# Mixture-of-experts layer: token rows of experts 3 to 7 turned by block transposes of VectorE instead of by TensorE and a PSUM copy

## The reference, cut to what matters

```python
h = h + attention(layernorm(h))          # h: [592, 256]
x = layernorm(h)
red = x @ w_red
wg_n = wg / jnp.maximum(jnp.linalg.norm(wg, axis=1, keepdims=True), 0.0001)
gates = jax.nn.softmax(red @ wg_n.T, axis=1)
idx = jnp.argmax(gates, axis=1)          # one expert of eight for each token
scores = jnp.take_along_axis(gates, idx[:, None], axis=1)
hid = gelu(einsum('td,edf->etf', x, w1) + b1)   # w1: [8, 256, 1024]
y = einsum('etf,efd->etd', hid, w2) + b2        # w2: [8, 1024, 256]
out = h + y[idx] * scores
```

## Time and profile before

| | |
|---|---|
| runs | 129.05 us median, 128.87 to 130.22 |
| profiled execution: its own time | 129.21 us |
| its span in the trace | 127.4 us, so 1.8 us lie around the span |
| mean granted clock of TensorE | 0.994 |
| PE busy / weight loads busy | 121.1 us (95%) / 102.5 us (80%) |
| DVE / ACT / POOL busy | 57.4 / 48.2 / 43.8 us |
| DMA | 32.75 MB, 257 GB/s over the span |

### The profile page before, as it was taken

How to read it: one execution, slowest core, us unless ns; L and a number is a source line. 1 busy time by engine, 2 the same in 40 slices (tenths; PEclk the granted TensorE clock), 3 DMA queues, 4 the chain that set the end, 5 groups by cost and what they waited for, 6 DMA issues and landing times.

```text
span 127.4 us, 3630 instructions
## 1 busy us (share of the span) xinstructions
PE 121.1 (95%) x1492; PEld 102.5 (80%) x1492; DVE 57.4 (45%) x181; ACT 48.2 (38%) x145; POOL 43.8 (34%) x59
## 2 busy tenths in 40 slices
PE   7999999999999999999999899999999999999970
PEld 2677888877667777788799798899898999999870
DVE  1140699581997858798887200160212121220220
ACT  0400002465575757575547660037233150606000
POOL 8800024590059029563858700032020202002052
PEclk9999999999999999999999999999999999999997
DMA  3999999139819999999999947999999999300011
GB/s 114 309 315 391 400 402 408 57 126 207 145 28 205 153 277 363 386 368 378 366 403 367 373 151 219 289 286 363 368 384 373 375 385 357 97 5 25 3 29 31
DMA packets 19697, 32.75 MB, mean 257 GB/s; under 512 B 1794, under 2 KB 13701, under 8 KB 19678
## 3 DMA queue, kind: packets, MB, share of 16 engines
q1 hardware_dynamic: 18126, 30.06, 73.2%
q0 software_dynamic: 784, 2.12, 4.6%
q10 hardware_dynamic: 768, 0.31, 0.9%
HBM read 27.41 MB, written 5.38 MB: 257 GB/s over the span
## 4 chain that ended last, share of the span: by engine, by line
PE 85%; DVE 5%; DMA 3%; issue 2%; POOL 1%; ACT 1%; POOLq 0%; SPq 0%; DVEq 0%
PE ps L838 20%; PE ps L854 19%; PE ps L548 11%; PE ps L695 5%; PE ps L609 4%; PE ps L708 4%; PE ps L739 4%; PE ps L602 4%; PE ps L677 4%; DMA early<-embed_in 3%; PE ps L702 2%; PE ps L819 2%; PE ps L635 2%; DVE wide L942 2%; PE ps L808 1%
## 5 line engine op out<-in xcount | busy, mean ns | idle before, releaser
L530 ACT ACTIVATE early<-ps,b1s 128x112 f32<-128x112 f32 x64 | 17.4, 355 | 30.4 <-PE ps L838 30.4
L838 PE MATMUL ps<-early,w1s 128*64 128x112 f32 x512 | 26.1, 259 | 0.5 <-issue 0.5
L838 PEld LDWEIGHTS ps<-early,w1s 128*64 128x64 f32 x512 | 25.6, 137 | 1.0 <-issue 0.8
L854 PE MATMUL ps<-w2s,early 128*64 128x256 f32 x224 | 25.7, 379 | 0.0
L854 PEld LDWEIGHTS ps<-w2s,early 128*64 128x64 f32 x224 | 20.0, 130 | 3.2
L548 PE MATMUL ps<-early 128*128 128x256 f32 x60 | 15.9, 415 | 0.2
L548 PEld LDWEIGHTS ps<-early 128*128 128x128 f32 x60 | 11.8, 205 | 3.5 <-DMA early<-embed_in 2.0
L1126 DVE COPY early<-ps 128x224 f32<-128x224 f32 x6 | 2.4, 392 | 24.4 <-PE ps L819 24.4
L1271 POOL DMA_INDIRECT out<-pos,early x4 | 3.8, 944 | 24.7 <-DVE pos L1144 24.4
L609 PE MATMUL ps<-xnt,wqkv 128*128 128x296 f32 x32 | 9.1, 422 | 0.0
L1271 POOL DMA_INDIRECT out<-pos,wide x3 | 2.9, 980 | 17.5 <-DVE pos L1144 17.5
(11 more groups left out here) (148 smaller groups left out, 183.4 us busy)
## 6 DMA issues: line engine op xcount, KB each, us to landing
w1s<-w SPq DMA_DIRECT2D x8, 1024.0 KB, 10.1
w2s<-w SPq DMA_DIRECT2D x8, 1024.0 KB, 12.8
early<-embed_in SPq DMA_DIRECT2D x5, 448.0 KB, 7.7
slot_scratch<-nil SPq DMA_DIRECT2D x1, 2240.0 KB, 14.1
early<-slot_scratch SPq DMA_DIRECT2D x4, 280.0 KB, 4.0
wide<-slot_scratch SPq DMA_DIRECT2D x4, 280.0 KB, 6.6
b2s<-b SPq DMA_DIRECT2D x4, 256.0 KB, 7.9
wqkv<-w_qkv SPq DMA_DIRECT2D x1, 768.0 KB, 10.9
```

The lines of the kernel that those rows point to most:

```text
L530: nc.scalar.activation(gt[:, t % 2, f, :], ps[:, 2 * (t % 2) + f // 4, (f % 4) * CAP:(f % 4 + 1) * CAP], ACT.Gelu, bias=b1t[:, f:f + 1]).t ...
L838: m = nc.tensor.matmul(ps[a * ROW_B:(a + 1) * ROW_B, 2 * (t % 2) + f // 4, (f % 4) * CAP:(f % 4 + 1) * CAP], w1s[:, r, k, c:c + ROW_B], xt ...
L854: m = nc.tensor.matmul(ps[n0:n1, 4 + t % 2, 0:D], gt[:, t % 2, f, n0:n1], w2s[:, r, f, :], start=(f == 0), stop=(f == FT - 1))
```

## The change

The identity matmuls and the PSUM copy stay for expert 2 alone, now inside down(1) before f = 6, into PSUM bank 0 (`turn_rows(ONCHIP)`). For experts 3 to 7 PE turns nothing. `rows_turned(t)` on DVE waits for the rows themselves and issues 16 transposes: each takes 32 token rows and, in one instruction, two blocks of 32 channels (one of each half of 128 channels), and writes a block [32 channels, 2, 32 tokens] of `xt`. `xt` becomes 128 tokens wide instead of 112. The row loads and the clearing take 128 rows of each expert instead of 112, so that the transposes read defined rows. Matmuls still use 112 tokens. down_halves no longer waits for `xt_ready`.

```diff
+QB = 32
+NQ = P // QB
...
-        xt = late(2 * KD * CAP).rearrange("p (b k n) -> p b k n", b=2, k=KD)
+        xt = late(2 * KD * P).rearrange("p (b k n) -> p b k n", b=2, k=KD)
...
+        def block_rows(t):
+            r = t % E
+            return rows[:, r, :] if r < RING else more[:, r - RING, :]
+
         def row_of(t):
-            r = t % E
-            return rows[0:CAP, r, :] if r < RING else more[0:CAP, r - RING, :]
+            return block_rows(t)[0:CAP, :]
...
-            sp.dma_start(of_expert[0:CAP, :, :], nil[0:CAP, :].unsqueeze(1).to_broadcast([CAP, E, ROW]))\
+            sp.dma_start(of_expert[0:P, :, :], nil[:, :].unsqueeze(1).to_broadcast([P, E, ROW]))\
               .then_inc(q["slots_cleared"], 16)
...
             def load_rows(t):
-                sp.dma_start(row_of(t), of_expert[0:CAP, t, :]).then_inc(gathered[t], 16)
+                sp.dma_start(block_rows(t), of_expert[0:P, t, :]).then_inc(gathered[t], 16)
...
             def turn_rows(t):
-                pe.wait_ge(gathered[t % E], 16 * (t // E + 1))
-                if t >= ONCHIP + 2:
-                    pe.wait_ge(q["xt_ready"], t - ONCHIP - 1)
+                pe.wait_ge(gathered[t], 16)
+                pe.wait_ge(q["gelu_ready"], FT * (t - 1))
...
-                        m = nc.tensor.matmul(ps[a * ROW_B:(a + 1) * ROW_B, 6 + t % 2, k * CAP:(k + 1) * CAP],
+                        m = nc.tensor.matmul(ps[a * ROW_B:(a + 1) * ROW_B, 0, k * CAP:(k + 1) * CAP],
...
                 for f in range(FT):
-                    if t == 1 and f == FT // 2:
-                        turn_rows(2)
+                    if t == 1 and f == FT - 2:
+                        turn_rows(ONCHIP)
...
             down(0)
             down(1)
-            turn_rows(3)
             hidden(2)
             for t in range(3, E):
                 hidden(t)
-                if t + 1 < E:
-                    turn_rows(t + 1)
                 down(t - 1)
...
             def rows_turned(t):
-                dve.wait_ge(q["xt_ps"], t - ONCHIP + 1)
+                dve.wait_ge(gathered[t % E], 16 * (t // E + 1))
                 dve.wait_ge(q["hidden_ps"], 2 * (t - 1))
-                V.tensor_copy(xt[:, t % 2, :, :],
-                              ps[:, 6 + t % 2, 0:KD * CAP].rearrange("p (k n) -> p k n", k=KD))\
-                    .then_inc(q["xt_ready"], 1)
+                z = block_rows(t)[:, D:2 * D].rearrange("p (k b) -> p k b", k=KD)
+                for i in range(NQ):
+                    for b in range(NQ):
+                        m = V.transpose(xt[b * QB:(b + 1) * QB, t % 2, :, i * QB:(i + 1) * QB],
+                                        z[i * QB:(i + 1) * QB, :, b * QB:(b + 1) * QB])
+                m.then_inc(q["xt_ready"], 1)
...
-            rows_turned(2)
+            dve.wait_ge(q["xt_ps"], 1)
+            V.tensor_copy(xt[:, 0, :, 0:CAP], ps[:, 0, 0:KD * CAP].rearrange("p (k n) -> p k n", k=KD)).then_inc(q["xt_ready"], 1)
             rows_turned(3)
             result(0)
             result(1)
```

More of the change, by code:

```diff
@@ L379, in _ @@
                 for i in range(OVF):
-                    sp.dma_start(of_expert[(i + 1) * CAP:(i + 2) * CAP, :, :], nil[0:CAP, :].unsqueeze(1).to_broadcast([CAP, E, ROW]))\
+                    sp.dma_start(of_expert[(i + 1) * P:(i + 2) * P, :, :], nil[:, :].unsqueeze(1).to_broadcast([P, E, ROW]))\
                       .then_inc(q["spill_cleared"], 16)
@@ L385, in _ @@
                     e = sp.value_load(meta[0:1, i:i + 1], min_val=0, max_val=E - 1)
-                    row = sp.value_load(meta[0:1, OVF + i:OVF + i + 1], min_val=0, max_val=(E + 1) * APART - CAP)
+                    row = sp.value_load(meta[0:1, OVF + i:OVF + i + 1], min_val=0, max_val=(E + 1) * APART - P)
                     r = (E + i) % RING
@@ L397, in _ @@
                     sp.wait_ge(scattered[i % 2], 16 * (i // 2 + 1))
-                    sp.dma_start(row_of(E + i), slot_d[bass.ds(row, CAP), :]).then_inc(gathered[i], 16)
+                    sp.dma_start(block_rows(E + i), slot_d[bass.ds(row, P), :]).then_inc(gathered[i], 16)
             sp.wait_ge(scattered[0], 16 * E // 2)
@@ L515, in _ @@
                 act.wait_ge(q["soon_ps"], KD * t + 1)
-                nc.scalar.activation(xt[:, t, 0, :], ps[:, BX[t][0], 0:CAP], ACT.Copy).then_inc(q["soon0_ready"], 1)
+                nc.scalar.activation(xt[:, t, 0, 0:CAP], ps[:, BX[t][0], 0:CAP], ACT.Copy).then_inc(q["soon0_ready"], 1)
             act.wait_ge(q["low_ready"], 1)
@@ L800, in down_halves @@
                 pe.wait_ge(q["y_ready"], t - 1)
-                pe.wait_ge(q["xt_ready"], t - ONCHIP + 1)
                 for h, bank in ((0, BHALF), (1, 4 + t % 2)):
@@ L839, in hidden @@
                                 ps[a * ROW_B:(a + 1) * ROW_B, 2 * (t % 2) + f // 4, (f % 4) * CAP:(f % 4 + 1) * CAP],
-                                w1s[:, r, k, c:c + ROW_B], xt[:, t % 2, k, :], start=(k == 0), stop=(k == KD - 1))
+                                w1s[:, r, k, c:c + ROW_B], xt[:, t % 2, k, 0:CAP], start=(k == 0), stop=(k == KD - 1))
                     if f % 4 == 3:
@@ L874, in _ @@
                     with pe.If(n > i):
-                        turn_rows(E + i)
                         hidden(E + i)
@@ L1096, in _ @@
                 dve.wait_ge(q["soon_ps"], KD * (t + 1))
-                V.tensor_copy(xt[:, t, 1, :], ps[:, BX[t][1], 0:CAP]).then_inc(q["soon1_ready"], 1)
+                V.tensor_copy(xt[:, t, 1, 0:CAP], ps[:, BX[t][1], 0:CAP]).then_inc(q["soon1_ready"], 1)
             scores_of(BY_PE, NT)
@@ L1119, in overflow @@
                 link(V.scalar_tensor_tensor(orow[:, :], obase[:, :], -float(CAP), orow[:, :], ALU.mult, ALU.add))
-                V.tensor_scalar(meta[:, OVF:2 * OVF], orow[:, :], float((E + 1) * APART - CAP), None, ALU.min)\
+                V.tensor_scalar(meta[:, OVF:2 * OVF], orow[:, :], float((E + 1) * APART - P), None, ALU.min)\
                     .then_inc(q["meta_ready"], 1)
             def rows_turned(t):
-                dve.wait_ge(q["xt_ps"], t - ONCHIP + 1)
+                dve.wait_ge(gathered[t % E], 16 * (t // E + 1))
                 dve.wait_ge(q["hidden_ps"], 2 * (t - 1))
-                V.tensor_copy(xt[:, t % 2, :, :],
-                              ps[:, 6 + t % 2, 0:KD * CAP].rearrange("p (k n) -> p k n", k=KD))\
-                    .then_inc(q["xt_ready"], 1)
+                z = block_rows(t)[:, D:2 * D].rearrange("p (k b) -> p k b", k=KD)
[4 more added lines that the diff above has]
+                m.then_inc(q["xt_ready"], 1)
             def result(t):
```

## The result

| | before | changed |
|---|---|---|
| median of 20 runs | 129.44 us | 128.66 us |
| ratio to before, 95% interval | | 0.9935 (0.991 to 0.996) |
| profiled execution, its span | 129.21, 127.4 | 129.17, 127.4 |

The change made the kernel faster by 0.65%, 0.84 us. The twenty runs of the kernel before, the first three of which the prediction started from, have a median 0.39 us above that of the three; the ratio applied to 129.05 would give 128.2, inside the range. But the gain is under half of the one forecast.

A forecast was written before the change was run, and what follows sets the result against it. The prediction took PE, busy 121.1 of 127.4 us and without a wait in the experts' stage, to bound the kernel. Its terms, -1.95 + 0.15 = -1.8 us, gave 127.3 us, range 126.7 to 128.6.

The forecast's parts named there:

- 1.95 us off TensorE: Experts' stage: removing turn_rows of experts 3 to 7 from PE, five times 0.39 us, saves 1.95 us.
- The start of hidden(2), 0.15 us: Before hidden(2): expert 2's copy has less PE work to cover it, costing 0.15 us more.
- The transposes of expert 3: Before hidden(3): 16 DVE transposes at 0.137 us take 2.2 us, ending 0.9 us before wanted; nothing on the path.
- 16 d - 3.1: Before hidden(3): PE's wait in us if the cover fails, with d the cost of one transpose.
- the first rival: Before hidden(3): transposes don't overlap, perhaps because a transposer fills before emptying; one wait of 0.6 to 1.1 us; chance 0.15.
- (N + 151)/0.96 ns: Expert 3's transposes: skill's tensor_tensor formula, estimating 0.224 us each; one behind another, a 0.5 us wait, run 127.8 us.
- Experts 4 to 7, nothing: Later periods: DVE needs 3.2 of 6.5 us for transposes and result steps, so nothing is added.
- DMA, nothing on the path: Clearing and row loads widened to 128 rows: clearing at most 1 us longer, weights covered by at least 0.7 us; nothing added.

The follow-up runs named there:

- e8: The changed kernel plus three extra transposes of 32, 128 or 256 elements behind those of experts 4 to 7; mean start distances 0.12, 0.22 and 0.35 us.
- e9: The changed kernel plus three extra transposes (unshifted, 128 partitions, bf16) or plain copies of 64 elements behind experts 4 to 7's; transposes start 0.145 us apart on the mean.
- e4: The changed kernel with one block transpose per expert instead of 16; ratio 0.9865 to the kernel before, stretch 45.67 us.
- e1: The changed kernel with clearing and row loads of 112 rows as before; ratio 0.9919 to the kernel before, stretch 46.16 us.
- e2: The kernel before with only the clearing and row loads widened to 128 rows; ratio 1.0021 to the kernel before, stretch 47.51 us.
- e13: The changed kernel with expert 2's copy on ScalarE, 112-row transfers and the two transpose loops swapped; ratio 0.9881 to the kernel before, stretch 44.72 us.
- e3: The changed kernel with expert 2's copy of turned rows on ScalarE instead of VectorE; ratio 0.9883 to the kernel before, stretch 45.58 us.
- e11: The changed kernel plus three extra 64-element transposes behind experts 4 to 7's; output, input or both in pieces 0.15 us apart, changing output partitions 0.25 us.
- e12: The changed kernel with its two transpose loops swapped, so four in a row write the same partitions; 16 take 3.97 us, ratio 0.9953 to the kernel before.
- e7: The changed kernel with each transpose split into two of one block, 32 per expert; they took 4.93 us, ratio 1.0026 to the kernel before.
- e15: The change itself, unaltered, measured a third time on chip 4; ratio 0.991 to the kernel before, stretch 45.49 us.
- e14: The changed kernel with no turns on TensorE, VectorE transposing expert 2 too, 112-row transfers and swapped loops; ratio 1.0038 to the kernel before.

## Why the prediction was wrong

- **1.95 us off TensorE**: right. Five turns are gone, and the period from hidden(4) to hidden(5) is 6.52 us (6.5 forecast).
- **The start of hidden(2), 0.15 us**: on the chain nothing is lost. From the start of down(0) to hidden(2) it was 82.84 - 75.16 = 7.68 and is 83.06 - 75.77 = 7.29, 0.39 less, the whole turn of expert 3.
- **The transposes of expert 3, "nothing on the path"**: this is the step that failed. The price was 0.137 us each, from a straight line through VectorE instructions of 5 and 256 elements on all partitions. The line is about right for neighbours on the same partitions (0.145 measured as the mean of 0.17 and 0.13). The 16 of a tile never are, and cost 0.25. The prediction's own formula, 16 d - 3.1, gives 0.9 us for it; 0.77 came. The mechanism and the place had been named, as the first rival; its price of 0.6 to 1.1 us holds the measured one. Its reason (a transposer that has to fill first) does not hold: transposes overlap if the partitions stay (e8, e9).
- **(N + 151)/0.96 ns** is what the Trainium skill (page "VectorE: DVE Perf Modes", section "The TRN2 errata — SBUF-src ops pay a fixed extra latency per instruction") states for an fp32 tensor_tensor; for 64 elements it gave an estimate of 0.224 us. For the transposes that would have been nearer than 0.137: the traces have a duration of 0.236 in the change, where each waits for the one before, and 0.191 where the partitions stay.
- **Experts 4 to 7, nothing**: right (e4), though with 0.35 us in hand at hidden(5) instead of 3.2, since the transposes took 4.0 us instead of 2.2 and result(2) waited (VectorE idle for 1.87 us) for the scatter of result(0), which the slow transposes of expert 3 had made late.
- **DMA, nothing on the path**: right in this stage (e1, e2, e13), open ahead of it, where the clearing landed 2.0 us later in the change's trace and not 1; w1 of expert 5 was issued at 83.09, landed 13.3 us later at 96.4, and was wanted at 99.5.
- The sum with the right price is -1.95 + 0.77 = -1.18 us, or 0.9% of the time, a ratio of 0.991. The three ratios of the change, 0.9935, 0.9831 and 0.991, scatter around that; the first, with the narrowest interval, has it at its edge. Whether a few tenths more were lost ahead of the stage is not shown.

## What to carry to other kernels

Before moving work from a full engine to an idle one, compute when its first result is wanted, not only its share of a period: here VectorE had room in every period, and still gave back 0.77 us of 1.95, once, at the first tile. Moving one copy of 0.39 us to another idle engine took the whole loss away (e3, and e13 to the hundredth). A price taken from other instructions must come from neighbours like the ones planned; where the sum has a threshold (here 0.2 us per transpose), the likeliest value on one side of it is not enough. And compare profiled executions from a point in the program that both share, not by their spans.

## What the hardware showed unexpectedly

- Transposes on VectorE on the same partitions as their neighbour start 0.13 to 0.17 us apart at 64 elements per partition; if the input's or the output's quarter of the partitions changes, 0.25 us, the full duration of the one before (e11, e12). At 32 elements: 0.12 on the mean in e8, 0.12 to 0.14 and 0.17 to 0.18 in turn in e7. Whether other operations than transposes behave so was not tried.
- A transpose on 128 partitions (four times the blocks) takes as long as one on 32 (0.50 and 0.48 us for three).
- On chips 2 and 3 TensorE paused in hidden(0) and hidden(1), between 70 and 76 us, for 1.6 to 2.1 us in several pieces that no wait explains, in the kernel with the order of before (e2) as in the changed ones. On the first chip it was 0.53 us (before) and 0.19 (changed), on chip 4 0.74 (e15), 0.53 (e13) and nothing (e12, e14). What this is stays open.
